# First slots of a decoder's self-attention: order of the first transfers, narrower waits, the function table, and the place of the output bias

## The reference

```python
q = (x @ Wq + bq).reshape(B, T, N_HEAD, hd).transpose(0, 2, 1, 3)
k = (x @ Wk + bk).reshape(B, T, N_GROUPS, hd).transpose(0, 2, 1, 3)
v = (x @ Wv + bv).reshape(B, T, N_GROUPS, hd).transpose(0, 2, 1, 3)
k = jnp.repeat(k, KV_PER_HEAD, axis=1)
v = jnp.repeat(v, KV_PER_HEAD, axis=1)
q_hat = q / (jnp.linalg.norm(q, axis=-1, keepdims=True) + EPS)
k_hat = k / (jnp.linalg.norm(k, axis=-1, keepdims=True) + EPS)
factor = (alpha * math.sqrt(hd)).reshape(1, N_HEAD, 1, 1)
q_scaled = q_hat * factor
...
```

## Time and profile before

| | |
|---|---|
| median of three executions | 1206.72 us (1205.46 to 1207.45) |
| span of the profiled execution, first to last instruction | 1198.9 us |
| what lies around the span, against the median | 7.8 us |
| TensorE busy | 1095.9 us (91%) |
| VectorE busy | 780.9 us (65%) |
| ScalarE busy | 588.6 us (49%) |
| GpSimd busy | 461.3 us (38%) |

### The profile page before, as it was taken

The page is one execution under the profiler, slowest core; times in us unless marked ns, Lnnn a source line. Parts: engine busy times, 40 slices in busy tenths (PEclk is TensorE's granted clock), DMA queues, the critical chain, the costliest instruction groups (busy, mean ns, idle before and its releaser), DMA issues.

```text
span 1198.9 us, 20821 instructions
## 1 busy us (share of the span) xinstructions
PE 1095.9 (91%) x7384; PEld 655.3 (55%) x7384; DVE 780.9 (65%) x1500; ACT 588.6 (49%) x1212; POOL 461.3 (38%) x756
## 2 busy tenths in 40 slices
PE   5999869999988598999879999899999999999997
PEld 3666635555553154777433455577786334545455
DVE  5999877888873412333666678676888465564655
ACT  2776617878767312333366555376874432121210
POOL 6999734666644163333225345451121000000001
PEclk7999969999989799999989999999999999999999
DMA  6965345666652122553504000010000000000000
GB/s 225 322 200 172 102 113 139 157 155 160 162 118 55 27 91 82 156 162 105 171 0 140 1 1 11 27 36 2 2 2 28 1 0 1 9 9 9 10 9 27
DMA packets 75354, 95.90 MB, mean 80 GB/s; under 512 B 12883, under 2 KB 62189, under 8 KB 74573
## 3 DMA queue, kind: packets, MB, share of 16 engines
q1 hardware_dynamic: 70835, 84.92, 25.3%
q0 software_dynamic: 3408, 9.34, 2.2%
q10 hardware_dynamic: 1010, 0.31, 0.1%
HBM read 57.47 MB, written 31.27 MB: 74 GB/s over the span
## 4 chain that ended last, share of the span: by engine, by line
PE 49%; ACT 5%; DVE 4%; DMA 4%; issue 3%; POOL 2%; POOLq 0%; SPq 0%; DVEq 0%; ACTq 0%
PE cps_h L2972 6%; PE cps_h L2141 4%; PE cps_h L1604 4%; DMA xrows<-c_xr,c_place_int 4%; PE cps_o L1623 3%; PE cps_h L2991 3%; PE cps_x L3005 2%; PE cps_x L3030 1%; PE cps_o L3030 1%; PE cps_t L2991 1%; PE cps_h L2603 1%; PE cps_o L2991 1%; PE cps_t L3005 1%; PE cps_x L2541 1%; PE cps_h L2586 1%
## 5 line engine op out<-in xcount | busy, mean ns | idle before, releaser
L902 DVE TENSOR_REDUCE b_nm<-a_s 128x4 f32<-128x1024 f32 x64 | 78.2, 1222 | 36.5 <-PE a_s L982 35.4
L2734 POOL TENSOR_SCALAR f_rstd<-f_mv 128x1 f32<-128x1 f32 x16 | 3.8, 240 | 252.9 <-DVE f_mv L2886 252.8
L937 ACT ACTIVATE a_late<-a_qkv 128x512 f32<-128x512 f32 x128 | 76.3, 596 | 45.0 <-PE a_qkv L1012 44.2
L2831 DVE TENSOR_TENSOR f_prod<-f_sg,f_kept 128x512 f32<-128x512 f32 (+1 forms) x48 | 33.2, 692 | 94.8 <-ACT f_kept L2762 90.8
L2972 PE MATMUL cps_h<-residT,w_f_w 128*128 128x512 f32 x176 | 80.8, 598 | 3.4 <-DVE f_inner L2868 1.9
L937 ACT ACTIVATE a_late<-a_y 128x512 f32<-128x512 f32 x128 | 76.4, 597 | 5.0 <-PE a_y L1012 3.4
L902 DVE TENSOR_REDUCE b_nm<-a_pt 128x4 f32<-128x1024 f32 x64 | 76.8, 1199 | 0.1
L2756 ACT ACTIVATE f_sg<-cps_h 128x512 f32<-128x512 f32 (+1 forms) x24 | 14.3, 596 | 123.6 <-PE cps_h L2991 107.6
L1027 PE MATMUL a_o<-a_late,b_vt 128*32 128x256 f32 x1024 | 70.1, 393 | 0.0
L1342 POOL DMA_INDIRECT routed<-c_out,c_target x39 | 37.5, 962 | 68.5 <-ACT c_out L1423 68.2
L2012 DVE SCALAR_TENSOR_TENSOR d_acc<-d_pad,d_cw,d_acc 128x512 f32<-128x512 f32 x72 | 58.4, 815 | 6.6 <-ACT d_acc L1913 4.9
(11 more groups left out here) (434 smaller groups left out, 2887.0 us busy)
## 6 DMA issues: line engine op xcount, KB each, us to landing
kparts<-a_rest SPq DMA_DIRECT2D x48, 192.0 KB, 3.4
a_rest<-a_rest SPq DMA_DIRECT2D x64, 128.0 KB, 3.1
xrows<-in_c_fill SPq DMA_DIRECT2D x13, 387.0 KB, 4.5
c_xrow<-xrows SPq DMA_DIRECT2D x39, 129.0 KB
c_back<-routed SPq DMA_DIRECT2D x16, 256.0 KB, 3.5
a_front<-kparts SPq DMA_DIRECT2D x12, 288.0 KB
a_front<-qparts SPq DMA_DIRECT2D x36, 96.0 KB
qparts<-b_xp SPq DMA_DIRECT2D x48, 64.0 KB, 2.5
```

The costliest lines, as they stand in the source:

```text
L902: dve.tensor_reduce(nm[s % 2][:, 4 * n:4 * n + 4].rearrange("p (g h) -> p g h", h=2), s1[step % 2][:], AX.X, ALU.max, negate=True).then_in ...
L937: act.activation(pr[g % 8][:], s2[g % 2][:], ACT.Exp, scale=SCALE).then_inc(s2_out, 1)
```

## The change

The weights go first in SP's queue; the bias row moves to the head of ScalarE's queue, followed by factor, cos and sin, which now share a semaphore with it (`bias_in`, 64 in all). VectorE waits for these four at its start, and no longer for `const` ahead of the loop. ScalarE runs one small Square on constants before the loop, which brings its function table load there. In slot 1 the output bias's matmuls on TensorE and its copy on ScalarE now stand behind the transposes of tile 0, and VectorE's split of it moves from slot 1 to slot 2.

```diff
-    consts = ((factor, "a_factor"), (cos, "cos"), (sin, "sin"), (k.headmask, "headmask"), (causal, "a_mask"),
-              (wo, "a_wo"), (borow, "a_bo"), (bvcol, "a_bvcol"))
+    turn_consts = ((factor, "a_factor"), (cos, "cos"), (sin, "sin"))
+    consts = ((k.headmask, "headmask"), (causal, "a_mask"), (wo, "a_wo"), (borow, "a_bo"), (bvcol, "a_bvcol"))
...
-        sp.dma_start(k.residT[:, :, 0:P], io["xT"][:, :, 0:P]).then_inc(first_in, 16)
-        sp.dma_start(biasrow[:], io["a_bias"][:, 0:NQK].broadcast_to([3, NQK])).then_inc(bias_in, 16)
         for dst, src in proj_consts:
             sp.dma_start(dst[:], io[src]).then_inc(proj_in, 16)
+        sp.dma_start(k.residT[:, :, 0:P], io["xT"][:, :, 0:P]).then_inc(first_in, 16)
         sp.dma_start(k.residT[:, :, P:CHUNK], io["xT"][:, :, P:CHUNK]).then_inc(x_in[0], 16)
...
     def scalar(act):
+        act.dma_start(biasrow[:], io["a_bias"][:, 0:NQK].broadcast_to([3, NQK])).then_inc(bias_in, 16)
+        for dst, src in turn_consts:
+            act.dma_start(dst[:], io[src]).then_inc(bias_in, 16)
         for dst, src in consts:
             act.dma_start(dst[:], io[src]).then_inc(const, 16)
+        act.wait_ge(k.built, BUILT)
+        act.activation(first_square[:], k.ones[:, 0:HD], ACT.Square)
...
+            if live(s - 1):
+                if s == 1:
+                    act.wait_ge(const, 16 * len(consts))
+                queries_keys(s - 1)
             if s == 1:
                 act.wait_ge(bo_full, 1)
                 act.wait_ge(bias_done, 1)
                 act.activation(bo_rows, o_ps[0:3, :], ACT.Copy).then_inc(bo_out, 1)
-            if live(s - 1):
-                if s == 1:
-                    act.wait_ge(const, 16 * len(consts))
-                queries_keys(s - 1)
...
-        dve.wait_ge(bias_in, 16)
+        dve.wait_ge(bias_in, 16 * (1 + len(turn_consts)))
...
-        dve.wait_ge(const, 16 * len(consts))
         for s in range(SLOTS):
...
-            if s == 1:
+            if s == 2:
                 split_output_bias()
...
+            if live(s - 4):
+                turn_y(s - 4)
+            if live(s - 1):
+                turn_queries_keys(s - 1)
             if s == 1:
                 pe.wait_ge(const, 16 * len(consts))
                 pe.matmul(o_ps, k.ones[0:1, :], borow[:], start=True, stop=False)
                 for c in range(KD):
                     ins = pe.matmul(o_ps, bvcol[:, c:c + 1].broadcast_to([P, P]), wo[:, c, :], start=False, stop=(c == KD - 1))
                 ins.then_inc(bo_full, 1)
-            if live(s - 4):
-                turn_y(s - 4)
-            if live(s - 1):
-                turn_queries_keys(s - 1)
```

More of the change, by code:

```diff
@@ L255, in self_attention @@
     factor, cos, sin = sb("factor", [P, H20]), sb("cos", [P, HD]), sb("sin", [P, HD])
-    causal = sb("causal", [P, T], BF16)
+    causal, first_square = sb("causal", [P, T], BF16), sb("first_square", [P, HD])
     qk, sq = front.many(2, [H20, HD]), front.many(2, [H20, HD])
```

## The result

| | before | after |
|---|---|---|
| median | 1201.99 us (1193.17 to 1207.86, 20 executions) | 1213.37 us (1200.48 to 1219.72, 20 executions) |
| ratio of the changed kernel to the one before | | 1.0075, 95% interval 1.0051 to 1.0098 |
| profiled execution: time, span | span 1198.9 | 1219.72, span 1217.9 |

The change makes the kernel slower by 0.75%, which is some 9 us. The ratio leaves out two of the changed kernel's 20 executions, those more than 1.5% above its fastest (1219.64 and 1219.72 us, the second is the profiled one), so it isn't the quotient of the two medians, 1.0095. The forecast was no change (1206.6 us) with a range up to 1209.2 us. The profiled execution of the changed kernel is one of its longest and that of the kernel before one of its shorter ones, so the 19 us between the two spans are not the price of the change; the ratio is.

The account below looks back on a forecast made before the run. TensorE, gapless from 60 to 90 us, was taken to bound self-attention, its dense stretch starting when rotate(2) ends (36.41). Terms -3.5 + 1.65 + 2.3 - 0.55 = -0.1 on the median of 1206.72 gave 1206.6 us, range 1203.4 to 1209.2.

Parts of the forecast that it names:

- Sin is small like the bias row but shares the engines with the weights; I take 4.9: Ahead of slot 0: sin, the last transfer VectorE waits for, lands at 4.9 us, bounds 4.35 and 5.8.
- tables late: Rival, ahead of slot 0: sin queues behind SP's transfers and lands near 8.3; +3.1 us, 1209.8 us; chance 8%.
- start: power of tile 0, against 14.78: Slot 0: GpSimd's power of tile 0 begins at 11.3 and not at 14.78, -3.5 us.
- from there to softmax(0): TensorE's bias matmuls: Slots 1 and 2: bias matmuls behind tile 0's transposes delay scores(0), softmax(0) at 27.6 and not 25.95, +1.65 us.
- split, softmax(0) to reciprocal: Slot 2, VectorE: the 3.06 us split ahead of rotate(2) finds only 0.77 us of idle time, +2.3 us.
- tail, reciprocal to end of rotate(2): End of rotate(2) on VectorE: 2.3 us and not 2.86, GpSimd's parts being done earlier, -0.55 us.
- Table load, weights first: Ahead of slot 0: the 1.28 us table load moves to where ScalarE is idle; weights first gains nothing.
- Late output bias: Slots 1 and 2: the moved bias matmuls cost +1.65 us and the moved split +2.3 us.
- gain kept: Rival, slots 0 to 2: earlier start stays and the split hides; rotate(2) ends at 33.3, -3.1 us, 1203.6 us; chance 12%.
- From tile 2 to the end: Everything behind tile 2's transposes, through layer 1, shifts by as much as the end of rotate(2), -0.1 us.
- later stages: Rival, behind tile 2: low-clock stretches fall otherwise, 1.7 us per projection, 3.4 for two, either direction; chance 10%.

Follow-up runs that it names:

- e2: The changed kernel with the output bias back in its old places on TensorE, ScalarE and VectorE: 1203.43 us against 1203.05, ratio 1.0009.
- e3: The kernel of e2 with the tables on their own semaphore, waited for one slot later: 1203.61 us against 1203.05, ratio 0.9995.
- e4: The changed kernel, output bias in its new places, with the tables on their own semaphore: 1203.92 us against 1203.05, ratio 1.0022.
- e9: The kernel of e3 with the context tile ahead of the rest of x and a second ahead of `resid`: 1199.11 us against 1203.93, ratio 0.9991.
- e12: The kernel of e9 with two unused reciprocals on VectorE in slot 7: 1205.01 us against 1205.58, ratio 1.0010.
- e1: The kernel before with only VectorE's split of the output bias moved to slot 2: 1209.65 us against 1203.05, ratio 1.0045.
- e5: The kernel before with only the output bias late on all three engines: 1208.78 us against 1204.65, ratio 1.0023.
- e6: The kernel before, unchanged, profiled a second time: 1206.14 us.
- e7: The kernel before, unchanged, profiled a third time: 1208.2 us.
- e10: The changed kernel, unchanged, profiled a second time: 1207.56 us, span 1205.7.
- e11: The changed kernel with one unused power of 128x4 on GpSimd in slot 7: 1206.88 us against 1205.58, ratio 1.0017.

## Why the prediction was wrong

The step that failed is **"Sin is small like the bias row but shares the engines with the weights; I take 4.9"**. It landed at 7.71, in e2 at 8.09, and the bounds that I gave it (4.35 and 5.8) don't reach there. They were taken from transfers that had no more than 128 KB of x ahead of them in their own queue, and not the weights beside them from the start. The rival "tables late" described what came, with its landing between 7.7 and 8.9 and its deciding point of 7.6, and I gave it 8%. It doesn't account for the size, though: by its own sum a landing at 7.71 is worth 7.71 - 4.9 - 0.2 - 0.1 = +2.5 us at tile 2, where 4.4 and 2.7 came, and some 9 in the total.

I had held the one-for-one count of packets of the earlier trace rows against this rival. That count stands between 8 and 12 us, and says how many packets passed, not how long a given small one took. The Trainium skill (DMA: Bandwidth & Descriptors, Queues, rings and completion order) says that an engine drains a whole packet of some 9 to 17 descriptors of one queue before it switches; by it I had written that the time would go towards 1209.8, and of the two readings this one came nearer. The late landing agrees with it, but no run here shows the order within an engine, so the landing is shown and its mechanism only argued. Two kernels in which the tables have their own semaphore say a little more: `cos`, as large as `sin` and issued half a microsecond before it, took 2.9 us from issue to landing in e3 and 2.8 in e4, and `sin` 7.2 and 5.8. A small transfer in that queue isn't late as such; the one that was waited for is.

Term by term, in the profiles:

| term of the sum | forecast | measured |
|---|---|---|
| start: power of tile 0, against 14.78 | -3.5 | +0.2 (14.98) |
| from there to softmax(0): TensorE's bias matmuls | +1.65 | +2.15 (16.82 against 14.67) |
| split, softmax(0) to reciprocal | +2.3 | +3.40 (7.50 against 4.10) |
| tail, reciprocal to end of rotate(2) | -0.55 | -1.37 (1.49 against 2.86) |
| sum | -0.1 | +4.4 |

- **Start.** Of the 3.7 us that are missing, 7.71 - 4.9 = 2.8 is the landing. The rest, about 1, is the bias work: it takes from 7.71 to 12.24, 4.5 us, and not 3.49, because it now falls beside GpSimd's parts of the first context tile (L550 1.16 us, before 0.71 for the same three). A second term would have failed even with `sin` at 4.9: I let GpSimd be free at 11.0 to 11.5, since its context tile is issued 0.5 earlier, but this tile came later in all profiles with the changed order (8.97 to 10.49 where it was 8.64), except e9 and e12, which issue it earlier still, and the power was at 12.18 in e4 and 13.27 in e3, with VectorE's squares long done. That the start waits for the tables alone is shown by e3 and e4, where their own semaphore puts the squares at 9.15 and 9.04.
- **Table load, weights first.** Right in mechanism: 1.28 us gone from slot 0, with ScalarE idle around it, and TensorE's first matmuls 1.2 us earlier for nothing.
- **Late output bias.** Right in sign and place, shown by e1 and e5, and too small. The transposes end at 23.2 and the bias matmuls at 26.3, which is 3.15 us as written; the scores then end at 31.7. Project(2) between them took 3.82 us, as at the low level in the earlier trace rows, so the clock had not risen earlier; I had taken the middle of both levels. The split takes 4.23 us and not 3.06, again beside GpSimd's parts, here of tile 3. The short tail of 1.49 is the other side of the same thing: GpSimd was done, as I had argued, and the 1.7 of the earlier trace rows was the nearer end and not the 2.3 that I took. Split and tail together were forecast as +1.75 and came as +2.0.
- **The rival "gain kept"** needed the split to end before 29.5. In e4, with the start mended, it ends at about 33.8, so it would have failed even without the tables. The start's gain of 2.6 us at the power in e4 is 0.2 at tile 2.
- **From tile 2 to the end.** The prediction let everything behind shift by as much as tile 2. That was the second wrong step. Up to the squares of tile 15 it about holds, when profiles in the same rhythm are compared: 137.7 and 134.6 in the changed kernel, 131.7 and 132.5 in e6 and e7, so 2.1 to 6.0 us later. The low clock behind TensorE's wait, which the rival "later stages" had, shows only in part. From tile 2 to these squares e6 and e7 take 95.7 us. The first profile of the changed kernel and e1, both with a granted clock of 0.66 from 40 to 50 us, take 96.8 and 96.7; but e10, e4 and e5, where the four matmuls of the projection behind the wait also took 2.1 to 2.5 us instead of 1.34, take 95.4 to 95.5, so nothing. The other 3 to 7 of the 9 us lie behind self-attention and stay open: the two profiles of the changed kernel differ by 9 us there, so one or two profiles can't place them. The record of all executions has a hint. The changed kernel's four shortest (1200.5 to 1202.8 us) have a granted clock of 0.970 to 0.973 on the mean of the whole span, its other sixteen (1208.3 us and more) 0.955 to 0.969. Whether the lower clock makes them longer or only marks waits elsewhere, no run tells.
- **What I read before.** The median of before fell from 1206.72 over 3 executions to 1201.99 over 20, and its profile shows 7.79 us per slot where 8.16 came in the two later ones. The 7.8 us that I set around the span mixed two executions: in the later runs time and span of one and the same execution are 1.8 to 2.1 apart (1219.72 and 1217.9, for one). The claim that TensorE works without a gap from 60 to 90 us holds only in the short rhythm. In the longer one VectorE is the engine without a gap, 29.4 of 30 us.

## What to carry to other kernels

When a small transfer is needed first, keep it on a semaphore of its own; joined to others that are issued after it, it is as late as the last of them, and behind large transfers that was 7.7 us instead of 3.7. Filler work belongs where its engine waits anyhow, and not ahead of an instruction on which two other engines depend: 3 us of small instructions moved by one slot cost some 0.45% (0.14 to 0.76). And follow a gain at the start to the next late transfer before counting it, and take a second profile of the unchanged kernel before taking a rhythm from one.

## What the runs showed of the hardware that I had not expected

**Two steady rhythms of one program.** The same loop settles at 7.79 or at 8.16 us per slot, the same program in either (the three profiles of before), and stays there. An added 1.09 us on GpSimd turned 8.17 into 7.79 (e11), an added 1.75 us on VectorE turned 7.79 into 8.17 (e12), each in one profile. What differs is which instructions of the two engines meet. The rows of e11 show it on VectorE's multiplication of 128x20, L494 (L491 in the changed kernel). There, at 39.84, with GpSimd idle, it takes 0.15 us; in e11 at 61.35 it takes 0.64, and ends at 61.99, just as GpSimd's subtraction, begun 0.18 earlier, ends at 61.97. L498 of e11 at 69.78, which takes 0.42 with GpSimd idle (L495 at 40.37), takes 0.89 and ends 0.28 behind GpSimd's L359 (70.67 and 70.39). Both end at the other's end plus their own time less 0.13 to 0.14 us. That reads rather like a wait for the other's end, in which only the first part of the instruction is already done, than like a slower run. The Trainium skill (SBUF — State Buffer, Who interferes with whom) says that a VectorE instruction with two inputs in SBUF contends with a GpSimd instruction that reads SBUF, and that the order of issue decides which of the two is blocked; these rows agree. GpSimd's power doesn't hold VectorE up in this way, though it reads SBUF too: in the changed kernel the two L484, with two inputs in SBUF each, take 0.54 us together at 38.83 with GpSimd idle, and 0.58 at 15.22, begun within the power that runs from 14.98 to 18.71. Why the same meetings return slot after slot, I haven't shown.

**A small transfer behind large ones.** `sin`, 8 KB and the fourth in its queue, was issued at 2.17 and was there 5.5 us later (in other profiles at 7.15 to 9.31), with 384 KB of weights and x in another queue issued from 0.72 on. `bvcol`, the last of nine, landed at 17.36 in e3, though its issue began at 4.87.
